# Expert outputs of a mixture-of-experts layer: scattered to two rows per token and summed, or added in memory by the transfers

## The reference

```python
x = _layernorm(x + attention(x))                       # no weights, eps 1e-5
# inner block, on x:
hidden_after_attn = x + attn_out @ proj_weight.T
z = ln(hidden_after_attn, ln2_weight, ln2_bias)        # 2048 tokens x 128
top_p, top_i = top_k(softmax(z @ router_weight), 2)    # weights of 2 experts, sum 1
# each expert takes up to 640 of its tokens, in order
exp_out = gelu(exp_in @ moe_w1) @ moe_w2               # 8 x 640 x 128
moe = zeros(2048, 128).at[padded_ids].add(exp_out * padded_probs)
x = _layernorm(x + hidden_after_attn + moe)            # eps 1e-5
```

## Time and profile before

| | us |
|---|---|
| time, median of 3 runs | 665.28 |
| the profiled execution | 662.71 |
| its span | 660.9 |

### The profile page before, as it was taken

The page is one execution under the profiler, slowest core; times in us unless marked ns, Lnnn a source line. Parts: engine busy times, 40 slices in busy tenths (PEclk is TensorE's granted clock), DMA queues, the critical chain, the costliest instruction groups (busy, mean ns, idle before and its releaser), DMA issues.

```text
span 660.9 us, 11452 instructions
## 1 busy us (share of the span) xinstructions
PE 535.9 (81%) x4355; PEld 286.7 (43%) x4355; DVE 406.1 (61%) x659; ACT 342.6 (52%) x662; POOL 194.9 (29%) x362
## 2 busy tenths in 40 slices
PE   4629999999999999989999999998932306999910
PEld 2302444444445454534455444453321204888710
DVE  1749877877797767798867799766053321222233
ACT  1710766766776867666766666676712111322303
POOL 4100331011125115114505004710406140445543
PEclk9955899999999999999999999998966556999965
DMA  6352123222322223222112122200100002433142
GB/s 151 95 160 56 48 62 106 83 84 80 112 88 67 95 74 109 62 82 70 51 45 60 53 75 65 65 24 2 34 16 32 0 13 65 129 109 103 56 135 64
DMA packets 49808, 47.61 MB, mean 72 GB/s; under 512 B 14442, under 2 KB 40020, under 8 KB 49755
## 3 DMA queue, kind: packets, MB, share of 16 engines
q1 hardware_dynamic: 45483, 36.97, 19.6%
q0 software_dynamic: 4272, 9.94, 4.4%
HBM read 31.86 MB, written 16.06 MB: 73 GB/s over the span
## 4 chain that ended last, share of the span: by engine, by line
PE 69%; DVE 15%; DMA 4%; ACT 3%; issue 3%; POOL 2%; SPq 2%; ACTq 0%; POOLq 0%; DVEq 0%
PE ps L669 32%; PE ps L707 16%; DVE row_max L1055 7%; PE ps L835 5%; PE ps L847 5%; PE ps L672 4%; PE ps L733 1%; DMA x_tok<-in_x 1%; DVE heads L1107 1%; DMA q_dram<-parts 1%; ACT probs L912 1%; PE ps L751 1%; PE ps L721 1%; DVE x_tok L1259 1%; DVE stats L1075 1%
## 5 line engine op out<-in xcount | busy, mean ns | idle before, releaser
L1055 DVE TENSOR_REDUCE row_max<-ps 128x1 f32<-128x1024 f32 x256 | 297.5, 1212 | 80.9 <-PE ps L672 42.0
L912 ACT ACTIVATE probs<-ps 128x512 f32<-128x512 f32 x512 | 268.0, 606 | 105.4 <-PE ps L672 66.1
L669 PE MATMUL ps<-k_stacks,q_stacks 96*128 96x512 bf16 x512 | 170.2, 399 | 24.1 <-DVE wv_t L1048 18.7
L669 PE MATMUL ps<-q_stacks,k_stacks 99*128 99x512 bf16 x512 | 164.6, 384 | 4.3 <-ACT probs L912 2.7
L707 PE MATMUL ps<-probs,v_unit 128*32 128x256 f32 x2048 | 124.4, 384 | 0.0
L672 PE MATMUL ps<-distance,slope_eye 128*128 128x128 bf16 x512 | 114.8, 224 | 0.0
L669 PEld LDWEIGHTS ps<-k_stacks,q_stacks 96*128 96x128 bf16 x512 | 44.6, 100 | 109.1 <-issue 43.4
L707 PEld LDWEIGHTS ps<-probs,v_unit 128*32 128x32 f32 x2048 | 60.3, 110 | 54.2 <-issue 10.8
L669 PEld LDWEIGHTS ps<-q_stacks,k_stacks 99*128 99x128 bf16 x512 | 48.9, 98 | 57.7 <-ACT probs L912 20.9
L672 PEld LDWEIGHTS ps<-distance,slope_eye 128*128 128x128 bf16 x512 | 50.7, 99 | 24.8 <-issue 1.4
L469 POOL COPY v_unit<-v_all 128x128 f32<-128x128 f32 x32 | 9.6, 303 | 163.0 <-PE ps L707 138.0
(11 more groups left out here) (162 smaller groups left out, 391.1 us busy)
## 6 DMA issues: line engine op xcount, KB each, us to landing
k_stacks<-k_dram SPq DMA_DIRECT2D x64, 144.0 KB
q_stacks<-q_dram SPq DMA_DIRECT2D x64, 72.0 KB
k_stacks<-in_c_alibi_k SPq DMA_DIRECT2D x32, 96.0 KB
w<-in_w SPq DMA_DIRECT2D x12, 256.0 KB, 3.0
xd<-blank POOLq DMA_DIRECT2D x8, 325.0 KB, 2.7
probs<-xd SPq DMA_DIRECT2D x8, 325.0 KB, 3.8
out_dram<-out_t SPq DMA_DIRECT2D x16, 128.0 KB
yt<-zeros POOLq DMA_DIRECT2D x4, 512.0 KB, 3.0
```

The source lines that it names most:

```text
L669: mm = pe.matmul(out, lhs, rhs, start=True, stop=not on_diagonal)
L912: act.activation(probs[:, k % KEPT, HALF * e:HALF * (e + 1)], ps[:, n % RING, :], ACT.Exp).then_inc(ring_read, 1)
L1055: dve.tensor_reduce(row_max[:, m % 2, i:i + 1], max_pair(k).rearrange("p a n -> p (a n)"), AX.X, ALU.max).then_inc(mx_used, 1)
```

## The change

`yt`, two rows for each token, becomes `acc`, one row for each token. SP writes the base (`x_tok`, four chunks of 256 KB, `keep_base`) to `acc` once a chunk's base is ready: chunk 0 in unit 15, chunk 1 in unit 23, chunks 2 and 3 behind the last heads. The 40 indirect transfers of the experts carry `compute_op=ADD`: they add their rows to `acc` in memory. As two experts can hold the same token, POOL waits before an expert's first transfer until all five of the expert before it have landed. At the end SP fetches `acc` (4 x 256 KB) into `x_tok`; the two additions on DVE, the zeros (one memset, four transfers) and `got` go. The root of the last norm is taken by ACT (Sqrt with eps as bias; one dummy Sqrt stands behind the last Gelu) and DVE's reciprocal instead of POOL. ACT scales the first two tiles of a chunk, DVE the other two.

```diff
-FILLS = EXPERTS + TOP * NT // 8
+FILLS = EXPERTS
@@ block.sync
+            def keep_base(c):
+
+                sp.wait_ge(base_ready, c + 1)
+                sp.dma_start(acc.rearrange("(a p) d -> p a d", p=P)[:, chunk(c), :],
+                             x_tok[:, chunk(c), :]).then_inc(acc_written, 16)
...
                 if m % 2 == 0 and m >= 2:
                     send_out(m // 2 - 1)
+                if m % UNITS_C == UNITS_C - 1 and UNITS_C < m < LAST * UNITS_C:
+                    keep_base(m // UNITS_C - 1)
             load_heads(LAST, 0, PAIRS_C - 1)
             send_out(PAIRS - 1)
             load_heads(LAST, PAIRS_C - 1, PAIRS_C)
+            keep_base(LAST - 1)
+            keep_base(LAST)
...
             for g in range(CHUNKS):
-                sp.dma_start(got[:, chunk(g), :], yt.rearrange("(a p k) d -> p a (k d)", p=P, k=TOP)[:, chunk(g), :]
+                sp.dma_start(x_tok[:, chunk(g), :], acc.rearrange("(a p) d -> p a d", p=P)[:, chunk(g), :]
                              ).then_inc(fetched[g], 16)
             for g in range(CHUNKS):
                 sp.wait_ge(normed, g + 1)
+                sp.wait_ge(normed_rest, g + 1)
@@ block.gpsimd
-                    pool.memset(zeros[:], 0.0).then_inc(late_set, 1)
+                    pool.memset(eps_column[:], EPS).then_inc(half_set, 1)
...
-                i, rows = m - 4 - EXPERTS, 8 * P
-                if 0 <= i < TOP * NT * P // rows:
-                    pool.dma_start(yt[i * rows:(i + 1) * rows, :].rearrange("(p a) d -> p (a d)", p=P),
-                                   zeros[:]).then_inc(filled, 16)
...
-            def body(e, u):
+            pool.wait_ge(acc_written, 16 * CHUNKS)
+            for e in range(E_):
+                u = e % 2
+
+
+                if e > 0:
+                    pool.wait_ge(y_sent[1 - u], 16 * CT * ((e + 1) // 2))
                 for a in range(CT):
...
                     pool.indirect_dma_start(
-                        out=yt, out_offset=bass.IndirectOffsetOnAxis(ap=y_to[u][:, a:a + 1], axis=0),
-                        in_=y_out[u][:, a, :], in_offset=None, bounds_check=TOP * NT * P - 1,
-                        oob_is_err=False).then_inc(y_sent[u], 16)
-
-            for e in range(E_):
-                body(e, e % 2)
-            for c in range(CHUNKS):
-                inverse_root(3, 2, c)
+                        out=acc, out_offset=bass.IndirectOffsetOnAxis(ap=y_to[u][:, a:a + 1], axis=0),
+                        in_=y_out[u][:, a, :], in_offset=None, bounds_check=NT * P - 1,
+                        oob_is_err=False, compute_op=ALU.add).then_inc(y_sent[u], 16)
@@ block.scalar
-            for c in range(CHUNKS):
-                act.wait_ge(scale_ready, c + 1)
-                for a in tiles(c):
-                    last = act.activation(x_tok[:, a, :], x_tok[:, a, :], ACT.Identity,
-                                          bias=shift[:, a:a + 1], scale=rstd[3][:, a:a + 1])
-                last.then_inc(normed, 1)
+            act.activation(root_table[:], eps_column[:], ACT.Sqrt)
+            for c in range(CHUNKS + 1):
+                if c < CHUNKS:
+                    act.wait_ge(var_ready[2], c + 1)
+                    act.activation(var_eps[3][:, chunk(c)], mv[2][:, chunk(c), 1], ACT.Sqrt,
+                                   bias=eps_column[:, 0:1]).then_inc(var_raised[3], 1)
+                if c > 0:
+                    k = c - 1
+                    act.wait_ge(scale_ready, k + 1)
+                    for a in tiles(k)[0:TC // 2]:
+                        last = act.activation(x_tok[:, a, :], x_tok[:, a, :], ACT.Identity,
+                                              bias=shift[:, a:a + 1], scale=rstd[3][:, a:a + 1])
+                    last.then_inc(normed, 1)
@@ block.vector
-            dve.wait_ge(base_ready, CHUNKS)
             for c in range(CHUNKS + 1):
                 if c < CHUNKS:
                     dve.wait_ge(fetched[c], 16)
-                    for k in range(TOP):
-                        done(dve.tensor_tensor(x_tok[:, chunk(c), :], x_tok[:, chunk(c), :],
-                                               got[:, chunk(c), k * D:(k + 1) * D], ALU.add))
+                    if c > 0:
+                        dve.wait_ge(var_ready[2], c)
                     norm_stats(2, x_tok[:, chunk(c), :], c)
                 if c > 0:
                     k = c - 1
-                    dve.wait_ge(rstd_ready[3], k + 1)
+                    dve.wait_ge(var_raised[3], k + 1)
+                    done(dve.reciprocal(rstd[3][:, chunk(k)], var_eps[3][:, chunk(k)]))
                     dve.scalar_tensor_tensor(out=shift[:, chunk(k)], in0=mv[2][:, chunk(k), 0], scalar=-1.0,
                                              in1=rstd[3][:, chunk(k)], op0=ALU.mult,
                                              op1=ALU.mult).then_inc(scale_ready, 1)
+                    for a in tiles(k)[TC // 2:]:
+                        last = dve.tensor_scalar(x_tok[:, a, :], x_tok[:, a, :], mv[2][:, a, 0:1], rstd[3][:, a:a + 1],
+                                                 ALU.subtract, ALU.mult)
+                    last.then_inc(normed_rest, 1)
```

More of the change, by code:

```diff
@@ L150, in body @@
         expert_rank, expert_base = sb("expert_rank", [P, TC * EXPERTS]), sb("expert_base", [P, TC * EXPERTS])
-        to_row = sb("to_row", [P, TOP, NT])
-        zeros, blank = sb("zeros", [P, 8 * D]), sb("blank", [P, CT, XW])
+        to_row = sb("to_row", [P, NT])
+        blank = sb("blank", [P, CT, XW])
         w1 = [sb(f"w1_{u}", [D, F]) for u in range(2)]
@@ L176, in body @@
         rest = qkv[:, 12:16, :].rearrange("p (b a) n -> p b (a n)", b=2)
-        got = qkv
         heads = sb("heads", [P, 2, 2, 2, QUARTER])
@@ L203, in body @@
         slot_u = [sb(f"slot_u{c}", [P, TOP, TC], U32) for c in range(CHUNKS)]
-        minus_half = sb("minus_half", [P, TC])
+        minus_half, eps_column = sb("minus_half", [P, TC]), sb("eps_column", [P, 1])
+        root_table = sb("root_table", [P, 1])
         flat = probs[:].rearrange("p a n -> p (a n)")
@@ L259, in body @@
         tile_full, tile_kept = sem("tile_full"), sem("tile_kept")
-        y_sent = [sem(f"y_sent{u}") for u in range(2)]
+        y_sent, acc_written = [sem(f"y_sent{u}") for u in range(2)], sem("acc_written")
         fetched = [sem(f"fetched{g}") for g in range(CHUNKS)]
-        normed, written = sem("normed"), sem("written")
+        normed, normed_rest, written = sem("normed"), sem("normed_rest"), sem("written")
         q_dram, k_dram, out_dram, max_dram = t["q_dram"], t["k_dram"], t["out_dram"], t["max_dram"]
-        xd, yt = t["xd"], t["yt"]
+        xd, acc = t["xd"], t["acc"]
         E_ = EXPERTS
@@ L490, in fetch @@
                     pool.memset(minus_half[:], -0.5).then_inc(half_set, 1)
-                    pool.memset(zeros[:], 0.0).then_inc(late_set, 1)
+                    pool.memset(eps_column[:], EPS).then_inc(half_set, 1)
                     pool.memset(blank[:], 0.0).then_inc(late_set, 1)
-                    pool.wait_ge(late_set, 2)
-                    pool.memset(blank[:, :, TO:TO + 1], float(TOP * NT * P)).then_inc(late_set, 1)
+                    pool.wait_ge(late_set, 1)
+                    pool.memset(blank[:, :, TO:TO + 1], float(NT * P)).then_inc(late_set, 1)
                     with nc.allow_non_contiguous_dma(reason="one value per partition"):
@@ L508, in fetch @@
                 if m == 4:
-                    pool.wait_ge(late_set, 3)
+                    pool.wait_ge(late_set, 2)
                 if 4 <= m < 4 + EXPERTS:
@@ L520, in fetch @@
                     for k in range(TOP):
-                        pool.tensor_copy(row_of[k][:, :, TO], to_row[:, k, :]).then_inc(rows_ready, 1)
+                        pool.tensor_copy(row_of[k][:, :, TO], to_row[:]).then_inc(rows_ready, 1)
             def inverse_root(i, src, c):
@@ L526, in inverse_root @@
                 if c == 0:
-                    pool.wait_ge(half_set, 1)
+                    pool.wait_ge(half_set, 2)
                 pool.tensor_scalar(var_eps[i][:, chunk(c)], mv[src][:, chunk(c), 1], EPS, None,
@@ L1301, in constants @@
                                np.tile(CAP * experts_ - EXPERTS * CAP, TC)]).astype(np.float32),
-        "c_to_row": (TOP * (P * np.arange(NT)[None, None, :] + np.arange(P)[:, None, None])
-                     + np.arange(TOP)[None, :, None]).astype(np.float32),
+        "c_to_row": (P * np.arange(NT)[None, :] + np.arange(P)[:, None]).astype(np.float32),
     }
@@ L1313, in program @@
     t["xd"] = nc.dram_tensor("xd", [EXPERTS * CAP, XW], F32).ap()
-    t["yt"] = nc.dram_tensor("yt", [TOP * NT * P, D], F32).ap()
+    t["acc"] = nc.dram_tensor("acc", [NT * P, D], F32).ap()
     body(nc, t)
```

## The result

| | median us | runs |
|---|---|---|
| before | 664.93 | 4 (664.22 to 665.90) |
| changed | 677.72 | 4 (675.56 to 678.51) |

The ratio on record is 1.0181, interval 1.0150 to 1.0211; the quotient of the two medians is 1.0192. The profiled execution of the changed kernel took 678.51 us, its span is 676.7 us.

What follows compares the result with a forecast made beforehand. The prediction took the stretch behind TensorE's last expert products as the bound, with POOL's queue setting its start. Wait +1.0, adding +1.8, fetch -0.8 and end -5.6 gave -3.6 us: 661.7 us, range 659.5 to 672.

Steps and rivals of the forecast that it cites:

- first rival: Experts' scatters: adding exceeds the 2.0 us slack, POOL sets the pace; upper ends give +12.3, 677.6 us; chance 0.20.
- D: Experts' scatters: extra landing time when adding, twice on the path; taken as 0.5 us, bounds 0 and 2.0.
- d: Experts' scatters: extra POOL issue time when adding, eight times on the path; taken as 0.1 us, bounds 0 and 0.43.
- the slack: Experts 1 to 6: 2.0 us each left within TensorE's 9.35 us period, of which adding would need 0.9.
- The wait itself: POOL between experts: about 0.1 us beyond the landing; hidden for experts 1 to 6, last expert +1.0 including landing.
- The fetch: SP's first chunk after the last scatter: 256 KB in place of 512, 3.2 us in place of 3.98, so -0.8.
- The end: DVE, ACT and POOL from first fetched chunk to last tile: 8.55 us in place of 14.15, saving 5.6.
- The close: From the last scaled tile to the span's end, last store and program close: 6.7 us, unchanged.
- The base stores and zeros: Before the experts: zeros leaving idle POOL and stores joining SP's queue cost 0, at most 0.3 us for chunk 2.

Runs made afterwards that it cites:

- e8: Changed kernel with adding transfers of 128 rows of 256 bytes instead of 512; one run, 673.61 us beside 666.62 for the kernel before.
- e9: Changed kernel with adding transfers of 64 rows of 512 bytes instead of 128 rows; one run, 667.06 us beside 666.62 for the kernel before.
- e10: Changed kernel as it stands, measured again on another chip: 676.26 us, ratio to before 1.0178.
- e12: Kernel before with roots on ACT/DVE, scaling partly shared, POOL taking some additions, ACT's dummy root told to wait for TensorE's last tiles: 659.35 us, ratio 0.9908.
- e1: Changed kernel with the addition taken out of the 40 transfers, wait between experts kept: 657.71 us, ratio to before 0.9867.

## Why the prediction was wrong

The forecast was 661.7 us, with 659.5 to 672.0 as its range and 0.21 on slower. The measured 677.72 lies above the range. It is nearly the 677.6 of the first rival, "adding is slow, and the chain of experts becomes the bound", and its mechanism is the one that the trace shows: POOL's pauses released by transfers. The agreement of the numbers is partly luck: it had D too large (2.0, measured 0.6 to 1.5), d (0.43, measured 0.58) and the wait (0.1, measured 0.75) too small, and left out the long first turn (+5.2) and the gain at the close (-3.8).

- **What adding costs in issue (the step that failed).** I took d = 0.1, with 0.43 as the upper end, "paid a second time". Measured: 1.549 - 0.974 = 0.58, beyond the bound. The bound came from the index part of a plain indirect issue, and nothing said that adding uses the same work twice; e8 and e9 show a price that is nearly fixed for each transfer. Eight times 0.58 is 4.6 us on the last two experts in place of 0.8, and the slack was gone: 4 x 0.58 = 2.3 for each expert, with 2.0 to spare. "Slack of the earlier experts needed: 0.5 + 4 x 0.1 = 0.9, under 2.0, so nothing there" is where the forecast broke: an expert's turn took 3.9 more than the 7.36 foreseen (2.3 of issue, 0.95 of landing, 0.65 of wait), 1.9 over the slack. Yet d alone would not have left the range: the first rival's formula with d = 0.58 and D = 0.5 gives +5.2, 670.4 us. The next three points did.
- **What adding costs in landing.** D = 0.5 proved the least of what is paid: the last landing took 2.71 against 2.08, +0.6. Behind experts 1 to 6 it was 2.7 to 3.7, 3.1 in the mean, so 0.5 to 1.5 more. I had also read the earlier trace rows as 2.1 to 2.2 and passed over its maximum of 3.4, which by itself takes 1.2 of the slack. What the page Collectives: The Full Stack of the Trainium skill says of a ReduceScatter's addition (The bandwidth ceiling: the fold count and why AG ≠ RS ≠ AR: two source reads) gives, as an estimate, 0.2 us more for the bytes of a transfer. The trace has more than that, and it does not go by bytes: with rows of half the bytes e8 still has 2.7 to 3.2 behind its experts 1 to 7. What the counts do show is the packet for each row. The page DMA: Bandwidth & Descriptors of the Trainium skill (Queues, rings and completion order) has 9 to 17 descriptors in a typical packet. If a row is one descriptor, which no run shows, the plain transfers' eight rows are just under that, and the adding ones' single row is far from it; that the packets are what makes the landing longer is not shown.
- **The wait itself.** I put 0.1 us on it; POOL's next issue starts 0.75 us after the landing (592.00 + 3.18 = 595.18, then 595.93). That could be read before: DVE's last tile of an expert ends at 573.46 + 1.38 = 574.84, and POOL's first issue behind it starts at 575.61, 0.77 later. Seven waits make 4.6 us. So an expert's turn is 4 x 1.85 + 3.1 + 0.75 = 11.25 us, which is the measured 11.26.
- **Expert 0 to expert 1.** 14.5 us, not 11.3. The last transfer of expert 0, issued at 577.59, landed after 6.3 us: SP issued the weights of expert 3 and the rows of expert 4, 837 KB, from 577.24 on. In e10 it was 5.1, in the same place. The next such meeting is that of the fifth transfer of expert 3 (614.55) with 512 KB of weights (614.51), and it has the longest landing of experts 1 to 6, 3.67. That the loads are the cause is read from these times; no run moved them. I had looked for a collision with the base stores and not with these loads, which stood in the trace.
- **The fetch:** 2.87 against 3.2 foreseen, -1.1 with its handover against -0.8.
- **The end:** 8.59 us from the first chunk to the last tile, against 8.55 foreseen. The order on DVE and ACT was as written down.
- **The close:** "which the change leaves as they are" was wrong by 3.8 us, in the change's favour. I subtracted the last tile from the span and did not ask what filled the difference; SP's wait of 4.2 us for the close was in the trace.
- **The base stores and zeros:** no difference that rises above the spread of the first scatter's start, which is 5 us and more; a smaller cost is not excluded.

With the measured stretches the sum reads +22.5 for the transfers, -1.1, -5.6, -3.8, together +12.0, next to +12.8 between the medians. From the +5.2 of d alone it comes there by the wait (seven times 0.65, 4.6 us), landings longer than the 2.65 us foreseen (2.8 us for experts 1 to 7, 3.6 for expert 0), and 4.1 us given back by fetch and close. The error was in taking the lower part of an unknown that no row priced, where the slack ended just above it and every expert behind that point paid.

## What to carry to other kernels

A price that no row shows has no upper end from a neighbour's row; where it is paid 40 times in one queue, measure one such instruction before building on it. A wait that is free alone and a dearer instruction that is free alone can use the same slack: add both up against the turn of the engine that sets the pace. And ask of the time between the last useful instruction and the end of the span which engine is the last to close.

## What the runs showed of the hardware

- An indirect transfer of 128 rows that adds in memory: 1.55 us of POOL (plain 0.97), 1.40 with 64 rows, the same with half the bytes a row; landing 2.7 us at best (plain 2.1); by the packet counts one packet for each row in place of one for each engine (8176 packets with 128 rows, 5616 with 64, 3696 plain). POOL's next issue starts 0.75 us after the landing that it waits for.
- POOL's closing drain ends 7.0 to 8.4 us after its last work, in all fourteen profiles. Work of 0.1 us on POOL at the end of a kernel cost 5.7 us.
- A table load is carried out ahead of the wait that stands before its activation (e12: the load at 631.71, the activation at 636.52).
- In the profiles of four kernels TensorE's last three tiles came up to 2.85 us apart, and in these and e1 each expert took some 0.2 us longer, with matmul records that show nothing of it; in the four the drain gives it away (6.9 in place of 2.2 us). The cause is open.
